# Attention keys turned to token-major by VectorE 32x32 blocks and a round trip through HBM instead of TensorE transposes, with the steps of the loop rotated

## What is computed

```python
def step(S, qkv):
    qb, kb, vb = qkv                      # one chunk of 128 tokens: 128 x 128 each
    attn = jnp.einsum('bhid,bhjd->bhij', qb, kb)
    attn = jnp.where(causal, attn, 0.0)
    o = jnp.einsum('bhij,bhjv->bhiv', attn, vb) + jnp.einsum('bhid,bhdv->bhiv', qb, S)
    S = S + jnp.einsum('bhid,bhiv->bhdv', kb, vb)
    return (S, o)
```

## Time and profile before

| | |
|---|---|
| time, median of 3 runs | 1179.42 us (1177.32 to 1179.82) |
| the profiled execution: first to last instruction | 1175.8 us |
| TensorE busy | 1140.9 us, 97% |
| VectorE busy | 826.4 us, 70% |
| ScalarE busy | 511.5 us, 44% |
| DMA queue of SyncE | 51.25 MB, 12.8% of the 16 DMA engines' time |
| the 64 attention steps | from about 28 to 665 us of the span |

### The profile page before, as it was taken

How to read it: one execution, slowest core, us unless ns; L and a number is a source line. 1 busy time by engine, 2 the same in 40 slices (tenths; PEclk the granted TensorE clock), 3 DMA queues, 4 the chain that set the end, 5 groups by cost and what they waited for, 6 DMA issues and landing times.

```text
span 1175.8 us, 21421 instructions
## 1 busy us (share of the span) xinstructions
PE 1140.9 (97%) x7620; PEld 1048.1 (89%) x7620; DVE 826.4 (70%) x1824; ACT 511.5 (44%) x1414; POOL 51.8 (4%) x70
## 2 busy tenths in 40 slices
PE   4999998999999999999999889999999999999998
PEld 3999997999988999989999879999999999999997
DVE  5666676666676666665645887778777777878777
ACT  5544644544544545445445633333333333333332
POOL 1000000000000000000000010202020202020100
PEclk9999999999999999999999999999999999999999
DMA  7101101001101011010001321102020201101010
GB/s 273 37 1 52 37 8 63 23 18 35 37 32 60 1 48 42 1 59 1 28 1 68 117 90 37 54 18 71 18 71 18 68 21 37 53 18 57 33 55 18
DMA packets 29542, 52.33 MB, mean 45 GB/s; under 512 B 2784, under 2 KB 21088, under 8 KB 29408
## 3 DMA queue, kind: packets, MB, share of 16 engines
q1 hardware_dynamic: 29456, 51.25, 12.8%
HBM read 35.95 MB, written 17.45 MB: 45 GB/s over the span
## 4 chain that ended last, share of the span: by engine, by line
PE 94%; DVE 3%; issue 1%; ACT 1%; DMA 1%; SPq 0%; DVEq 0%
PE ps L212 67%; PE ps L539 5%; PE ps L573 5%; PE ps L553 4%; PE ps L579 4%; PE ps L532 2%; PE ps L484 2%; PE ps L658 2%; PE ps L602 1%; PE ps L670 1%; PE ps L459 1%; DMA work<-in_L_attn_Wv 1%; DVE work L1182 0%; DVE work L1077 0%; DVE onT L1018 0%
## 5 line engine op out<-in xcount | busy, mean ns | idle before, releaser
L212 PE MATMUL ps<-r_k,r_gate_up 128*128 128x512 f32 x768 | 188.0, 395 | 4.3 <-DVE work L1222 4.3
L212 PEld LDWEIGHTS ps<-r_k,r_gate_up 128*128 128x128 f32 x768 | 141.3, 188 | 32.3 <-DVE work L1222 4.8
L212 PE MATMUL ps<-hT,r_q 128*128 128x512 f32 x384 | 101.6, 400 | 6.8 <-issue 5.2
L212 PE MATMUL ps<-r_o,onT 128*128 128x256 f32 x768 | 107.3, 289 | 0.8 <-DVE onT L1018 0.8
L212 PEld LDWEIGHTS ps<-r_q,r_v 128*128 128x128 f32 x768 | 100.5, 193 | 5.9 <-issue 2.0
L212 PE MATMUL ps<-hT,r_k 128*128 128x512 f32 x384 | 105.6, 410 | 0.0
L212 PE MATMUL ps<-r_q,r_v 128*128 128x256 f32 x768 | 104.2, 286 | 0.0
L212 PE MATMUL ps<-r_v,hT 128*128 128x512 f32 x384 | 104.0, 407 | 0.0
L212 PEld LDWEIGHTS ps<-r_o,onT 128*128 128x128 f32 x768 | 95.7, 190 | 2.1 <-DVE onT L1018 2.1
L899 ACT ACTIVATE r_v<-work 128x512 fp32r<-128x512 f32 x64 | 40.5, 632 | 131.3 <-DVE work L1222 131.3
L789 ACT ACTIVATE work<-ps 128x128 f32<-128x128 f32 x256 | 67.4, 278 | 64.5 <-PE ps L579 64.5
(11 more groups left out here) (130 smaller groups left out, 2109.6 us busy)
## 6 DMA issues: line engine op xcount, KB each, us to landing
work<-kept SPq DMA_DIRECT2D x17, 514.0 KB, 4.5
work<-in_L_attn_hidden_states SPq DMA_DIRECT2D x16, 512.0 KB, 4.5
kept<-work SPq DMA_DIRECT2D x9, 514.0 KB, 3.6
work<-kept_xq SPq DMA_DIRECT2D x9, 512.0 KB, 3.3
kept_xq<-work SPq DMA_DIRECT2D x8, 512.0 KB, 2.9
out<-work SPq DMA_DIRECT2D x7, 512.0 KB, 3.5
work<-raw SPq DMA_DIRECT2D x6, 352.0 KB, 3.0
quant<-work SPq DMA_DIRECT2D x6, 352.0 KB, 2.3
```

The costliest lines, as they stand in the source:

```text
L212: done = pe.matmul(out_ap, a, b, start=first and n == 0, stop=last and n == 2, skip_group_check=skip)
```

## The change

It does four things.

1. The four transposes of `kT` on TensorE and ScalarE's copy into `k_tok` go. In their place VectorE transposes the 32x32 blocks of `kT` with one instruction (`block_k`) into a new tile `k_blocks`, whose innermost order is feature, then chunk. SyncE stores that to HBM (`move_k`, one DMA of 128x4x128) and, after the state shares of the running step are done, loads it back in four DMAs of 32 partitions (`load_k`), which puts the blocks in their places. `k_tok` is now laid out as (token, feature, chunk), so the state shares read their weights `k_tok[:, :, c]` with a step of 4 elements (16 bytes).
2. The order of a step on TensorE becomes: scores, K projection, Q projection, ds, `turn_o`, V projection, o, output projection. The turn of h moves to the end of step h = 3, behind the output projection, and uses B_TURN instead of B_K.
3. The loop is rotated by two steps (`ROLL = 2`): its body runs from step 2 of a batch to step 1 of the next, and the last step of a batch is followed by an ordinary first step. On VectorE the FP4 scales of the weight piece move from h = 2 to h = 3, `turned_lo` in h = 3 moves behind `o_norm`, and `residual` of both halves stands in h = 1.
4. At the start the K weights come before the Q weights, and the three copies of FP4 weights inside HBM are issued by GpSimd after the last projection weight is there. The causal mask has one chunk, broadcast over four.

The core of the diff:

```diff
-        H_BANKS = (B_K, B_SCORE)
+        H_BANKS = (B_TURN, B_SCORE)
+        LAG, ROLL = 1, 2
...
-        k_tok = one.cut(CH, P)
+        k_tok = one.cut(P, CH)
...
+        k_blocks = one.cut(QUADS, CH * QUAD)
...
+                def move_k(value, again=True):
+
+                    if again:
+                        sp.wait_ge(k_tok_loaded, 16 * QUADS * (value - 1))
+                        sp.sem_inc(passed_sp, 1)
+                    sp.wait_ge(k_blocks_ready, value)
+                    sp.sem_inc(passed_sp, 1)
+                    sp.dma_start(k_moved.rearrange("b p x -> p b x"), k_blocks).then_inc(k_moved_out, 16)
+                    sp.wait_ge(k_moved_out, 16 * value)
+                    sp.sem_inc(passed_sp, 1)
+
+                def load_k(value):
+                    for q in range(QUADS):
+                        sp.dma_start(k_tok[q * QUAD:(q + 1) * QUAD].rearrange("p (a d) c -> p a (d c)", a=QUADS),
+                                     k_moved[q].rearrange("(a p) x -> p a x", a=QUADS)).then_inc(k_tok_loaded, 16)
...
+                    if not (final and j == STEPS - 1):
+                        move_k(t0 + j + 2)
+                        sp.wait_ge(ds_done, t0 + j + 1)
+                        sp.sem_inc(passed_sp, 1)
+                        load_k(t0 + j + 2)
...
-                        pe.wait_ge(k_ready, t0 + j + 1)
-                        for c in range(CH):
-                            done = pe.transpose(ps[:, B_TURN, c * P:(c + 1) * P], kT[:, c * P:(c + 1) * P],
-                                                ident[:, :])
-                        done.then_inc(k_turned, 1)
...
+                    if not (final and last):
+                        project(wk, B_K, h_next, s_next, k_done)
+                        pe.wait_ge(v_ready, min(CH, STEPS - j) + t0 + j if final else t0 + j + CH)
+                        project(wq, B_Q, h_next, s_next, q_done)
+                    pe.wait_ge(k_tok_loaded, 16 * QUADS * (t0 + j + 1))
...
+                        done = pe.matmul(ps[:, B_STATE, c * P:(c + 1) * P], k_tok[:, :, c],
+                                         v_sb[:, half, c, hv:hv + P], start=True, stop=True)
...
+                    if h == CH - 1 and ahead:
+                        pe.wait_ge(h_ready, n0 + s + 2)
+                        turn_h(0)
+                        turn_h(1)
...
-                        act.wait_ge(k_turned, t0 + j + 1)
-                        act.activation(k_tok, chunks(ps[:, B_TURN, :]), ACT.Copy).then_inc(k_tok_ready, 1)
...
+                        act.wait_ge(k_blocks_ready, t0 + j + 1)
+                        copy_k(t0 + j + 2)
+                        copy_q(t0 + j + 2, (j + 1) % 2)
...
+                def block_k(value):
+
+                    dve.wait_ge(k_ready, value)
+                    dve.transpose(k_blocks.rearrange("p b (d c) -> p b c d", c=CH),
+                                  kT.rearrange("p (c b t) -> p b c t", b=QUADS, t=QUAD)).then_inc(k_blocks_ready, 1)
...
+                    if not (final and j == STEPS - 1):
+                        dve.wait_ge(k_moved_out, 16 * (t0 + j + 1))
+                        block_k(t0 + j + 2)
+                    dve.wait_ge(ds_done, t0 + j + 1)
...
+                    if h == CH - 1 and ahead:
+                        turned_lo(0, 1 - s, n * KD + KD + 1)
+                        turned_lo(1, 1 - s, n * KD + KD + 2)
```

More of the change, by code:

```diff
@@ L594, in _ @@
-                with pe.Fori(0, batches - 1) as b:
-                    attention(b, False)
-                attention(batches - 1, True)
+                    h, s = j % H, j // H
+                    h_next, s_next = (j + 1) % H, ((j + 1) // H) % HALVES
+                    last = j == STEPS - 1
+                    ahead = not (final and s == HALVES - 1)
+                    pe.wait_ge(k_ready, t0 + j + 1)
+                    pe.wait_ge(q_ready, t0 + j + 1)
+                    if h == CH and ahead:
+                        pe.wait_ge(hT_ready, (n0 + s) * KD + 2 * KD)
@@ new lines, in attention @@
+                    if not first or j:
+                        turn_o(t0 + j)
+                    if ahead or h < CH:
+                        pe.wait_ge(q_ready, t0 + j + 2)
+                        values(*((1, h, s) if h < CH else (0, h - CH, 1 - s)))
+                    pe.wait_ge(attn_ready, t0 + j + 1)
+                    for c in range(CH):
+                        region = ps[:, B_O, c * P:(c + 1) * P]
+                        alone = s == 0 and c == 0
+                        done = pe.matmul(region, attn[:, c, :], v_sb[:, half, c, hv:hv + P],
+                                         start=True, stop=alone)
+                        if not alone:
+                            before = carry[:, h, :] if c == 0 else state[:, c - 1, :]
+                            if c:
+                                pe.wait_ge(state_ready, b * UPDATES + updates_before(j) + c)
+                            done = pe.matmul(region, qT[:, j % 2, c * P:(c + 1) * P], before,
+                                             start=False, stop=True)
@@ new lines, in attention @@
+                    done.then_inc(o_done, 1)
+                    if not first or j:
+                        if (j - 1) % H == 0:
+                            pe.wait_ge(x2_summed, n0 + s + 1)
+                        out_projection((j - 1) % H, t0 + j)
+                    if h == CH - 1 and ahead:
+                        pe.wait_ge(h_ready, n0 + s + 2)
+                        turn_h(0)
+                        turn_h(1)
+                for j in range(ROLL):
+                    attention(0, j, True, False)
@@ L598, in turn_activations @@
+                with pe.Fori(0, batches - 1) as b:
+                    for j in range(ROLL, STEPS):
+                        attention(b, j, False, False)
+                    for j in range(ROLL):
+                        attention(b + 1, j, False, False)
+                for j in range(ROLL, STEPS):
+                    attention(batches - 1, j, False, True)
                 def turn_activations(r, banks=TURN_BANKS):
@@ L873, in _ @@
-                with act.Fori(0, batches - 1) as b:
-                    attention(b, False)
-                attention(batches - 1, True)
+                    h, s = j % H, j // H
+                    last = j == STEPS - 1
+                    ahead = not (final and s == HALVES - 1)
+                    if not (final and last):
+                        act.wait_ge(k_blocks_ready, t0 + j + 1)
+                        copy_k(t0 + j + 2)
+                        copy_q(t0 + j + 2, (j + 1) % 2)
+                    if not first or j:
+                        o_hi(t0 + j)
@@ new lines, in attention @@
+                    if h == CH + 3 and not final:
+                        fp4_round(w4_piece, w4_scale, mine).then_inc(piece_ready, 1)
+                    if h == 2:
+                        x2_factor(n + 1, mine)
+                    if h == CH - 1 and ahead:
+                        turned_lo(0, 1 - s, n * KD + KD + 1)
+                        turned_lo(1, 1 - s, n * KD + KD + 2)
+                    if h == CH - 1:
+                        wgate_up_lo(b, s)
+                for j in range(ROLL):
+                    attention(0, j, True, False, before)
@@ L1174, in settled2 @@
+                for j in range(ROLL, STEPS):
+                    attention(batches - 1, j, False, True, last_batch)
                 def settled2(ins, mine):
```

356 lines of the change are left out of this document (147 added, 209 removed).

## The result

The changed kernel took 1221.3 us (median of 4 runs, 1220.51 to 1222.99), the kernel before on the same chip 1178.63 us (1177.32 to 1179.82): ratio 1.036 (95% interval 1.035 to 1.037). It is slower, and by more than the whole range allowed. The profiled execution has a span of 1219.3 us (its own time 1221.05), 43.5 us more than before. Here 1.75 us lie around the span, and 1.6 to 1.8 us in the other executions; so the profiled execution of the kernel before took about 1177.6 us (an estimate), and the 3.6 us that the prediction put around its span are too many.

What follows compares the result with a forecast made beforehand. The prediction took TensorE, busy 97% of the span, as the bound. Gains of 25.0 (transposes), 2.2 (ends of batches) and 0.8 (start) less 18.9 (turn of h) gave 9.1 us off 1179.4: 1170.3 us, range 1158 to 1197.

Steps and rivals of the forecast that it cites:

- The weight loads of ds: 448 TensorE loads reading k_tok with a 16-byte step: cost taken as 0, bounds 0 to 49 us.
- case (a): Rival: strided weight loads of ds show and the kernel is slower, 1195 us at half, 1219 at full; chance 0.22.
- The transposes: Four key transposes a step leave TensorE: 0.39 x 64 = 25.0 us gained, bounds 22.4 to 27.5.
- What the prediction feared: Q projection, now ahead of ds, takes 1.48 us instead of 1.40, cutting the transposes' gain to 22.4 us.
- The turn of h: TensorE waits for turned_lo on VectorE before the scores of h = 4: 7 x 2.7 = 18.9 us lost (14 to 25).
- case c: Rival: each of seven waits brings a dip of TensorE's clock, 7 us more, 1177 us, no change; chance 0.05.
- The way of the keys: Store to HBM and four loads back before the next step's ds: 6.7 of 9.4 us, hidden with 2.7 to spare.
- up to 4 us: At the start, the first trip of the keys beside three big HBM copies: priced at 0, loss possible to this size.
- up to 1.4: VectorE's block transpose of the keys: 0.69 us expected, this many us if its 16-byte-step writes run at half speed.
- Ends of batches and start: Waits for o_norm and o_lo go, 2.2 us gained; first Q projection's wait covered, 0.8 gained; jumps' issue idle stays.
- its sum: Main case, all terms added for the whole kernel: 9.1 us off 1179.4, 1170.3 us; chance 0.53.

Runs made afterwards that it cites:

- b_stride2: The kernel before with only the layout of k_tok changed, two chunks side by side, so ds weights are read with an 8-byte step: 1181.94 us, ratio 1.003.
- b_nokeys: The kernel before without the four key transposes on TensorE and ScalarE's copy of them, so ds is not of the real keys: 1153.19 us, ratio 0.977.
- a_pieces_turnback: The changed kernel with keys packed in k_tok (128-byte pieces in HBM) and the turn of h back between turn_o and V projection: 1159.49 us, ratio 0.983.
- a_turnback: The changed kernel with the turn of h back between turn_o and the V projection, turned_hi and turned_lo moved along: 1200.74 us, ratio 1.018.

## Why the prediction was wrong

**The weight loads of ds are the step that failed.** The prediction took 0 from bounds of 0 and 49 us, "because the overlap of the pair is the nearest row". The runs show the upper end: 10.22 - 9.37 = 0.85 us in the 32 steps with eight pairs, 9.98 - 9.37 = 0.61 in the 32 with six, 46.7 us in all. The overlap was real but the wrong thing to read: b_stride4 is the kernel before with this layout alone, and its steps are longer by the same 0.85 and 0.61 us. Pairs followed each other at 0.11 us with no idle time, and the page showed loads busy 89% of the span beside matmuls of 97%: there was little room for a longer load, and case (a) said so itself ("a slower load has little room"). How little, the runs show: a load 5 ns longer (b_stride2) made a pair some 5 ns longer, one 133 ns longer made it 107 ns longer. With that sentence, 0 should have been the end of the range and not its middle. Case (a) at its full price, 1219 us, named the cause and, within 2.3 us, the time. The cause is shown; that the time is so near is in part luck, since 11.5 us of clock and 2.4 us of the last step, which it did not hold, were made up by terms that came out more favourably (the transposes, the turn of h, the ends of batches, the start) and by a stride that cost 46.7 and not 49.

The Trainium skill's rule that the prediction set against the layout ("SBUF — State Buffer", section "Door 1: The DMA port swizzle") holds: the same note wants at least two hits in a 16-byte line for full bandwidth, and the loads took 196 ns at two (8-byte step), 249 in the mean at 1.33 (12 bytes, with one load in seven packed) and 324 at one. The rule gave the direction, which the prediction set aside; it gives no size, so it would have spoken for case (a) and not for its 1219 us.

**The transposes**: 25.0 gained was forecast; b_nokeys gives 9.82 - 9.38 = 0.44 us a step, 28 us over 64, the upper end. What the prediction feared does not come: Q ahead of ds takes 1.38 us (257.75 to 259.13) and not 1.48. K, which stands behind the scores in both kernels, takes 1.48 in both.

**The turn of h**: 7 x 2.7 = 18.9 forecast, measured are seven waits of 2.17 to 2.25 us. A step with a turn is 13.43 us, of which 10.22 are an ordinary step and 0.88 the eight transposes (10.70 - 9.82 before), so 2.33 are lost, and another 0.1 in the next step: 7 x 2.43 = 17.0 us. The chain over VectorE that the prediction counted is the one that released the scores (`hT L1027`): `o_norm` and the two passes of `turned_lo` follow each other on VectorE without idle time. Mechanism and size hold, within the range of 14 to 25.

**The clock** (case c) was priced at 1 us for each turn of h. A dip costs 1.6, and it does not follow every wait: 3 of 7 turns, but also the first trip, both jumps and the last step. Seven more dips than before are 11.5 us between the two profiled executions, a cost that no term of the sum had. Not all of that need be the change's: the profiled execution of before had a mean granted clock of 0.999, while 36 of the 40 executions of before beside the experiments had 0.993 to 0.997, with spans 0.5 us shorter to 3.6 us longer. As an estimate from those clocks (0.003 to 0.004 of 1176 us, at 1.7 us for 3.4 us at half clock), the usual execution of before has two or three such dips too.

**The way of the keys**: 6.7 us forecast. In after the store is issued at 106.02, the loads at 108.47, and with 1.3 us until the fourth is issued and 2.1 to land they are there at 111.9: 5.9 us, and ds begins at 115.52. Hidden, as forecast. What the prediction missed is the last step. It has no projection of a next head between scores and ds, so 3 us of cover are gone, and ds waits 2.42 us. The first trip is not hidden either; its 1.69 us lie inside the "up to 4 us" that the prediction left open. The blocks took 1.11 us instead of 0.69, inside the "up to 1.4" and near the 1.24 us that it set beside them, and apart from the turn of h TensorE did not wait for VectorE in the loop.

**Ends of batches and start**: the waits at the ends went, about 1.2 us a batch instead of 0.7; the "issue" at the jumps stayed (2.72 and 3.06 us; before 2.79 and 2.38), in this execution with a dip behind it. At the start the scores of step 1 begin at 37.01 instead of 38.16, although the first trip's wait and a dip lie ahead of them.

The account against the span, in us: stride +46.7, transposes -28.2, turn of h +17.0, dips +11.5, last step's wait +2.4, ends of batches -3.7, start -2.8 (1.15 earlier, with 1.6 of a dip that is counted among the seven). That is +42.9 against 43.5 measured.

One slip of the prediction changed nothing here: its bounds (22.4 to 27.5, 14 to 25, up to 4 at the start) give 1163 to 1183 us for its sum, and not 1160 to 1177.

## What to carry to other kernels

Where pairs of a weight load and a short matmul (here 128x128x128 in fp32) already follow each other without a gap, do not count on the overlap to hide a slower load: here 107 of its 133 ns showed. Price it at its upper end. Keep at least two fp32 elements of such a read in each 16-byte piece; a layout that makes a transfer easier may be paid for by every reader. A chain over another engine wants independent work of its own length between its start and its reader, and the last round of a loop, where that work is missing, has to be priced by itself.

## What the runs showed of the hardware

- An fp32 weight load of 128x128 took 191 ns packed, 196 with an 8-byte step, 324 with 16 bytes and 331 with 32. A pair of load and matmul went from 0.110 to 0.217 us, at 12 bytes to 0.163.
- Writers take longer too: ScalarE's copy of 128x512 took 590 ns packed, 631 with 8 bytes, 1085 with 16 and 1127 with 32. VectorE's block transpose of 128x512 in fp32 took 707 ns packed and 1106 with 16-byte steps.
- A store cut in four with 128-byte pieces costs the queue more. In a_pieces_turnback the four stores are 2.59 us of issue, 0.65 each against 0.38 for the one store in after with 512-byte pieces, and the loads follow 4.34 us after the first of them, against 2.45 in after. Which share is the number of stores and which the size of the pieces, no run tells:

```profile
108.83 2.59 SPq L342 DMA_DIRECT2D k_moved<-work  x4
113.17 1.74 SPq L348 DMA_DIRECT2D work<-k_moved  x4
```

- Waits of 1.7 to 3.1 us were followed in some cases by some 3.4 us at clock 0.50, which costs 1.6 us, in others not; behind the second jump of a_turnback (2.89 us) the stretch was twice as long and cost 2.9. In the profiled execution of before, neither jump of the loop (2.79 and 2.38 us idle) had one; in after and in b_nokeys both had. The length of the wait does not decide it: in b_stride2, in the order of before, 2.29 us at the first jump had a dip and 2.69 at the second had none. Here is the stretch behind the first jump before:

```profile
190.00:196.00 6.00, 4.59 (x28) 4.03 (x29) 0.74 (x1) 1.27 (x3) 0.00 (x0) 1.00 0.39 109
```

Since the mean granted clock also differs between executions of one and the same kernel (0.993 to 0.999 in 40 of before), a difference of one or two dips between two profiles says nothing about a change. What decides for or against a dip stays open; no run here tells it.
